# Gated cross-attention and block-sparse FFN on one core: tile 0's row maxima put into its queries by TensorE, w1's load issued without a wait, low parts of the FFN weights on GpSimd

## The reference, cut to what matters

```python
x = x + tanh(g_xattn[0]) * xattn(layernorm(x), ctx, ctx)      # 16 heads of 16, causal softmax
x = x + tanh(g_ffn[0]) * ffn(layernorm(x), w_router, b_router, w1, b1, w2, b2)

# ffn
prob = softmax(xf @ w_router + b_router); idx = top_k(prob, 4)   # mask over 16 blocks
h = relu(xf @ w1.T + b1)          # 256 -> 1024
y = (h * mask) @ w2.T + b2        # 1024 -> 256
```

## Time and profile before

| | us |
|---|---|
| median of 3 runs | 681.2 (681.01 to 684.17) |
| the profiled execution, its own time | 680.97 |
| its span in the trace | 679.1 |
| TensorE busy | 659.7 (97%) |
| GpSimd busy | 556.0 (82%) |
| ScalarE busy | 538.9 (79%) |
| VectorE busy | 527.8 (78%) |

### The profile page before, as it was taken

How to read it: one execution, slowest core, us unless ns; L and a number is a source line. 1 busy time by engine, 2 the same in 40 slices (tenths; PEclk the granted TensorE clock), 3 DMA queues, 4 the chain that set the end, 5 groups by cost and what they waited for, 6 DMA issues and landing times.

```text
span 679.1 us, 30579 instructions
## 1 busy us (share of the span) xinstructions
PE 659.7 (97%) x12960; PEld 611.9 (90%) x12960; DVE 527.8 (78%) x1429; ACT 538.9 (79%) x785; POOL 556.0 (82%) x718
## 2 busy tenths in 40 slices
PE   6779999999999999999999999999999999999997
PEld 5668899999999999999999999989999999999997
DVE  6899887788777778788778878777878877877742
ACT  4668788888888888888888888888888888887732
POOL 6677888988988898888898898888888889887643
PEclk9899999999999999999999999999999999999999
DMA  5323355556545446645556654544554554553110
GB/s 197 96 55 86 88 109 99 116 109 115 120 114 116 99 110 116 111 112 113 100 117 107 116 111 122 103 107 114 113 113 112 116 100 96 98 86 64 28 40 32
DMA packets 192279, 69.24 MB, mean 102 GB/s; under 512 B 166160, under 2 KB 191888, under 8 KB 192144
## 3 DMA queue, kind: packets, MB, share of 16 engines
q1 hardware_dynamic: 191312, 65.72, 45.7%
q10 hardware_dynamic: 832, 1.57, 0.6%
HBM read 19.03 MB, written 8.39 MB: 40 GB/s over the span
## 4 chain that ended last, share of the span: by engine, by line
PE 86%; DVE 5%; DMA 3%; ACT 2%; issue 2%; POOL 1%; SPq 1%; POOLq 0%; DVEq 0%
PE bank L423 11%; PE score_banks L344 10%; PE bank L357 8%; PE score_banks L314 8%; PE bank L425 8%; PE bank L424 8%; PE bank L446 8%; PE bank L447 8%; PE bank L448 8%; PE bank L371 4%; PE bank L401 2%; PE score_banks L327 1%; DMA used_all<-used 1%; PE bank L393 1%; ACT weights L525 1%
## 5 line engine op out<-in xcount | busy, mean ns | idle before, releaser
L880 POOL TENSOR_TENSOR h_low<-hid,h_high 128x512 fp32r<-128x512 f32 x128 | 164.2, 1283 | 12.8 <-ACT hid L560 12.8
L738 DVE SCALAR_TENSOR_TENSOR hid<-bank,b_cols,used_all 128x256 f32<-128x256 f32 x248 | 108.1, 477 | 65.9 <-PE bank L425 58.2
L873 POOL TENSOR_SCALAR_AFFINE_SELECT weights<-weights 128x1024 f32<-128x1024 f32 x128 | 138.2, 1103 | 18.2 <-ACT weights L525 16.4
L423 PE MATMUL bank<-xT_high,w_high 128*128 128x256 f32 x496 | 151.5, 305 | 0.8 <-DVE hid L738 0.7
L525 ACT ACTIVATE weights<-score_banks 128x1024 f32<-128x1024 f32 x128 | 124.3, 1024 | 34.7 <-PE score_banks L344 34.6
L424 PE MATMUL bank<-xT_low,w_high 128*128 128x256 f32 x496 | 139.4, 281 | 0.0
L425 PE MATMUL bank<-xT_high,w_low 128*128 128x256 f32 x496 | 139.4, 281 | 0.0
L446 PE MATMUL bank<-w_high,h_high 128*128 128x256 f32 x488 | 137.3, 281 | 0.7 <-POOL h_low L880 0.7
L447 PE MATMUL bank<-w_low,h_high 128*128 128x256 f32 x488 | 137.7, 282 | 0.0
L448 PE MATMUL bank<-w_high,h_low 128*128 128x256 f32 x488 | 136.2, 279 | 0.0
L423 PEld LDWEIGHTS bank<-xT_high,w_high 128*128 128x128 f32 x496 | 93.3, 188 | 8.9 <-DVE hid L738 1.1
(11 more groups left out here) (105 smaller groups left out, 1411.1 us busy)
## 6 DMA issues: line engine op xcount, KB each, us to landing
x_in<-in_x SPq DMA_DIRECT2D x31, 256.0 KB, 3.1
out_y<-y_out SPq DMA_DIRECT2D x31, 256.0 KB, 2.2
c_in<-in_ctx SPq DMA_DIRECT2D x30, 256.0 KB, 2.8
qT<-qT SPq DMA_DIRECT2D x128, 4.0 KB
w_stage<-in_w1T ACTq DMA_DIRECT2D x1, 1024.0 KB, 9.2
hid<-in_w2T SPq DMA_DIRECT2D x8, 128.0 KB, 2.7
kT_parts<-k_parts SPq DMA_TRANSPOSE x57, 2.8
qT_parts<-q_parts SPq DMA_TRANSPOSE x57, 2.7
```

What stands on the lines that cost most here:

```text
L423: pe.matmul(out=bank, lhsT=w1_high[:, k, c], rhs=high, start=k == 0, stop=False)
L738: dve.scalar_tensor_tensor(hid[:, n % 4, j], hid_bank(n)[:, j * TOKS:(j + 1) * TOKS], b1_cols[:, c:c + 1], used_all[:, p % 2], ALU.add, AL ...
L873: pool.affine_select(out=w, in_=w, compare_op=ALU.is_ge, fill=0.0, base=0, pattern=[[0, 2 * HB], [1, S]], channel_multiplier=-1).then_inc( ...
L880: pool.tensor_tensor(h_low[:, p % 2, chunks], hid[:, n % 4], h_high[:, p % 2, chunks].bitcast(F32), ALU.subtract).then_inc(h_low_made, 1)
```

## The change

For tile 0 the maxima no longer ride. VectorE writes them to a tile of their own, `first_ride` (zeroed at the start by one more memset). TensorE first copies tile 0's queries into the free bank M1 by a matmul with the identity (`first_again`, 128x512, in iteration -1), then adds the maxima into them there by eight accumulating matmuls (`first_maximum`, in iteration 0 behind scores(1)), and ScalarE copies the bank to `qT` (`first_evacuated`). `shifted_scores(0)` waits for this copy instead of the DMAs, `max_row(0)` is gone, and q_transposed(2) moves behind scores(1) and `first_maximum`. ScalarE issues w1's load without the wait for x. The pieces of the weights are made one in iteration 0, two each in 1, 2 and 3 and one in 4, and GpSimd subtracts all eight; VectorE's `weights_low` is gone.

```diff
+        first_ride = sb("first_ride", [P, HB, U, PAD], F32)
...
         def pieces_of(i):
-            return {0: (0, 1), 1: (2, 3), 2: (4, 5), 3: (6,), 4: (7,)}.get(i, ())
-        W_LOW_BY_POOL = (0, 2, 4)
+            return {0: (0,), 1: (1, 2), 2: (3, 4), 3: (5, 6), 4: (7,)}.get(i, ())
...
             def q_transposed(b):
                 pe.wait_ge(qn_made, b + 1)
-                if b >= MAX_LAG:
+                if b > MAX_LAG:
                     pe.wait_ge(max_found, b - MAX_LAG + 1)
...
+            def first_again():
+                pe.wait_ge(q_copied, 1)
+                pe.matmul(out=banks[M1][:], lhsT=ident[:], rhs=qT[:, 0, :], start=True, stop=False)
+
+            def first_maximum():
+                pe.wait_ge(max_found, 1)
+                for r in range(HB):
+                    f, t = divmod(r, 2)
+                    for g in range(2):
+                        turned = pe.matmul(out=banks[M1][:, r * S + g * HALF:r * S + (g + 1) * HALF],
+                                           lhsT=first_ride[:, 2 * t + g].rearrange("p u d -> p (u d)"),
+                                           rhs=ident[:, f * HALF:(f + 1) * HALF], start=False,
+                                           stop=r == HB - 1 and g == 1)
+                turned.then_inc(first_turned, 1)
...
             def shifted_scores(b):
-                pe.wait_ge(max_landed[s], 2 * 16 * (b // TS + 1))
+                if b == 0:
+                    pe.wait_ge(first_copied, 1)
+                else:
+                    pe.wait_ge(max_landed[s], 2 * 16 * (b // TS + (1 if s else 0)))
...
-                    pe.wait_ge(w_low_made, 2)
-                    pe.wait_ge(w_low_also_made, 2)
+                    pe.wait_ge(w_low_made, 4)
...
                     if i + 2 >= 0:
                         k_transposed(i + 2)
                         q_transposed(i + 2)
+                    if i + 1 == 0:
+                        first_again()
                 else:
-                    if q_early(i + 2):
+                    if i > 0 and q_early(i + 2):
                         q_transposed(i + 2)
...
                     if i == 0:
+                        first_maximum()
+                        q_transposed(i + 2)
                         k_transposed(i + 2)
...
+            def first_evacuated():
+                act.wait_ge(first_turned, 1)
+                act.copy(qT[:, 0, :], banks[M1][:]).then_inc(first_copied, 1)
...
-            act.wait_ge(x_landed[1], 16)
             act.dma_start(w1_stage[:].rearrange("p k e c r -> p k (e c r)"),
...
                 elif i >= 0:
+                    if i == 0:
+                        first_evacuated()
...
-                ride = q_pad[:, carrier % QS, :, RIDE_COL].rearrange("p (t g u) -> p u t g", g=2, u=U)
+                if b == 0:
+                    dve.wait_ge(first_zeroed, 1)
+                    ride = first_ride[:, :, :, MAX_COL].rearrange("p (t g) u -> p u t g", g=2)
+                else:
+                    ride = q_pad[:, carrier % QS, :, RIDE_COL].rearrange("p (t g u) -> p u t g", g=2, u=U)
...
-            def weights_low(i):
-                for n in (n for n in pieces_of(i) if n not in W_LOW_BY_POOL):
-                    _w, stage, high, low = w_piece(n)
-                    dve.wait_ge(w_high_made, n + 1)
-                    dve.tensor_tensor(low, stage, high.bitcast(F32), ALU.subtract).then_inc(w_low_also_made, 1)
...
-                    dve.wait_ge(w_low_made, 3)
-                    dve.wait_ge(w_low_also_made, 5)
+                    dve.wait_ge(w_low_made, 8)
...
+            dve.memset(first_ride[:], 0.0).then_inc(first_zeroed, 1)
...
-                weights_low(i)
                 if not early and 0 <= i - 2 < N:
...
             def weights_low(i):
-                for n in (n for n in pieces_of(i) if n in W_LOW_BY_POOL):
+                for n in pieces_of(i):
...
-                if 0 <= i < N:
+                if 1 <= i < N:
                     max_row(i)
```

More of the change, by code:

```diff
@@ L170, in build @@
         tri_made = sem("tri_made")
+        first_zeroed, first_turned, first_copied = (sem(n) for n in ("first_zeroed", "first_turned", "first_copied"))
         numbers_set, filler_set = sem("numbers_set"), sem("filler_set")
@@ L182, in build @@
             "top_found", "clipped_made", "clipped_found", "marked_made"))
-        w_low_also_made = sem("w_low_also_made")
         gated_b2_made, adding_made = sem("gated_b2_made"), sem("adding_made")
@@ L438, in ffn_out @@
                     pe.wait_ge(q_copied, QUERIES_BY_PE)
-                    pe.wait_ge(w_low_made, 3)
-                    pe.wait_ge(w_low_also_made, 5)
+                    pe.wait_ge(w_low_made, 8)
                 if t == 0:
```

## The result

688.89 us (688.21 to 690.21), against 681.95 for the kernel before in the same comparison: ratio 1.0102, interval 1.0081 to 1.0123. So the change makes the kernel 7 us slower. I had named 682.5 and a range up to 684.3. The profiled execution took 688.39 us.

A forecast was written before the change was run, and what follows sets the result against it. TensorE was taken to bound the kernel from 70 to 600 us, so a later start moves the end equally. Profiled 680.97 us plus 1.5 of router lateness, start's gain included, gave 682.5, range 680.0 to 684.3.

The forecast's parts named there:

- w1's load: ScalarE's issue at the start: from 6.58 to about 4.9 us, sharing engines with x's tiles, cost 0 to 1, taken 0.
- Rival 3: At the start, w1's load delays x's tile 4; from 0.75 us late it decides, 1.5 us gives 684.0; chance 0.07.
- the start's gain: Tile 0's second scores start at 15.3 instead of 16.07, 0.75 us; about 0.95 us ahead at iterations 1 and 2.
- the sign of being wrong: At the start, x's tile 4 landing well after 12.5 us would show the prediction wrong.
- SyncE's released loads: Loads of context, x and w2 go out from about 8.6 instead of 15.0 us; nobody needs them until iteration 2.
- The low parts: GpSimd's subtractions, 1.3 us each, ahead of roots in iterations 1 to 4 delay xn; router 0.8 to 2.2 us late, taken 1.5.
- The clock: From 17 to 21 us it should stay up, winning up to 0.5 us more, of which 0.2 was kept.
- Rival 1, 2 and 4: Start's gain survives: 680.0, chance 0.20. Hold-ups of VectorE in iterations 3, 4 add: 683.7, 0.12. Nothing net: 681.0, 0.11.
- the hold-up rival: GpSimd subtractions hold up VectorE in iterations 3 and 4: 1.5 + 0.7 + 0.5 us, 683.7; chance 0.12.

The follow-up runs named there:

- c3: Kernel before without the wait ahead of w1's load and with x's tiles 4 to 7 issued first, maxima and low parts as before: 681.75 us, ratio 0.9990.
- a2: Kernel before with only the wait ahead of w1's load taken away: 685.21 us, ratio 1.0045.
- b4: Changed kernel, w1's load still without a wait, with x's tiles 4 to 7 issued directly behind tiles 2 and 3: 684.83 us, ratio 1.0019.
- b3: Kernel before with tile 0's maxima by TensorE, SyncE waiting in iteration 0 for tile 2's query copy before later loads: 682.79 us, ratio 1.0003.
- a1: Kernel before with only tile 0's maxima put in by TensorE, w1's wait and low parts as before: 684.01 us, ratio 1.0033.
- b2: Changed kernel with TensorE's idle time filled by transposes of the identity ahead of early second scores and xn transposes: 689.82 us, ratio 1.0093.
- b1: Changed kernel with GpSimd's low parts put behind the next iteration's roots instead of ahead of them: 688.07 us, ratio 1.0077.
- c1: Changed kernel with x's tiles 4 to 7 issued first and low parts in new places, split between GpSimd and VectorE: 681.11 us, ratio 0.9988.
- c2: Changed kernel with x's tiles 4 to 7 issued first and all low parts on GpSimd behind the next iteration's roots: 682.04 us, ratio 0.9997.
- a4: Changed kernel with the wait ahead of w1's load put back: 687.27 us, ratio 1.0080.
- a3: Kernel before with only the low parts moved, all on GpSimd, one, two, two, two, one pieces: 687.34 us, ratio 1.0071.

## Why the prediction was wrong

- **w1's load: the step that failed.** I wrote that the issue would go "from 6.58 to about 4.9" and gave it "cost 0 to 1 us, I take 0". It left at 3.52, 2 us ahead of x's tiles 4 to 7. Then, not the transfer, but the issue on the other queue was held: 4.04 us for a load of 8 KB. I had priced two transfers sharing the engines, which c3 shows to cost nothing, and not one queue's issue being held by another's. The cost that I took as 0 was 3.1 us alone (a2), and the reordering that removes it from the changed kernel gives 5.7 us (b4). The Trainium skill, Perfetto Trace Analysis, DMA Instruction — HWDGE (DVE, Sync), says that the duration shown for such an issue holds first the wait for a descriptor generator that two sequencers share (it names VectorE's and SyncE's and notes that the pair is the compiler's choice; here it would be ScalarE's and SyncE's), then its use. A wait for w1's own issue doesn't fit the trace: that issue ended at 3.93, two loads of 0.1 KB went out behind its start in the usual 0.89 us (3.65 to 4.54), and the held one began at 4.58. That w1's early issue causes the hold is shown (a2 differs from before in nothing else); what in the path holds it is open. Rival 3 named the right victim, x's tile 4, with a bound of 0.75 us for losing the start's gain and a price of 684.0; the landing was 2.8 us late, which is also the sign of being wrong that I had named.
- **The start's gain: right in the trace once x is in time, in part by luck.** Predicted 0.75 us at tile 0 and 0.95 at tiles 1 and 2; b4 shows 0.7 and 1.2, b3 0.54 at tile 0 and, behind the stall, 0.7 late at tile 1. I had the second scores wait for VectorE's maxima. In b4 these ended at 14.47, as x came even earlier than before, and the second scores started at 15.35 behind TensorE's own queries and keys: `first_maximum` took 2.00 us and not 1.6. In the time no run shows this gain.
- **SyncE's released loads: wrong in general.** That "nobody needs them until iteration 2" missed that w1 shares the engines with them: a1 against b3, 2 us. In the changed kernel w1 left early enough (landed at 14.4); whether these loads slowed x's landing there, no run separates.
- **The low parts: right mechanism, sized well only at full clock.** 0.95 ahead to 1.5 behind is 2.45 us. b4 shows 1.2 ahead to 1.8 behind, 3.0. In the changed kernel it was 4.25, with TensorE idle behind xn and its clock fallen; in b2, at full clock, the same stretch is 3.3 longer than before (24.73 us). I had the wait of xn in iteration 4; the one in iteration 2 I called "level", and it was 1.57 us.
- **The clock.** I expected it to stay up from 17 to 21 us, as the idle time would be filled. It was 2.5 us of idle time again, for x instead of the maxima, and fell again. The trace of b2 puts its worth at some 2 us, its time can't tell it from nothing.
- **Rival 1, 2 and 4.** The start's gain survived in no kernel with the low parts ahead of the roots. VectorE's xn took 0.80 us at 34.95 and 51.05, beside GpSimd's x2_b2, as the hold-up rival had it, but that is 0.4 us each, not the loss; beside a low part it took 1.20 us (b1).

## What to carry to other kernels

A wait can have a second duty: the wait ahead of w1's load kept x's issue ahead of it, and the maxima's DMAs kept w2's loads behind it. Before taking one away, list what stands behind it on its queue and what on the other queues goes out in that time, and order urgent loads ahead of bulk ones by program order instead. On an in-order engine move work behind the short instruction that others wait for (here the roots), not just onto an engine with less busy time; and measure a start-up change tile by tile, since the sum of its parts tells little. And a profile is one execution: executions of the kernel before alone lie between 679.96 and 685.66 us beside c1, so a difference of 1 or 2 us between two traces needs many executions behind it.

## What was not expected of the hardware

- A load of 1 MB issued on ScalarE's queue held an issue on SyncE's for 4.04 us (after), both loads of that line for 4.22 us (a2) instead of 0.90 us. It was not the next issue but the third behind it. With x's loads ahead of it the same two loads took 1.13 us (c3), 2.08 (b4) and 2.82 (c2).
- A DMA of ScalarE's queue was issued at 3.52 us, ahead of four copies that precede it in the program (3.62 to 4.86 us).
- TensorE stalls within `attention_out(0)` until 3.2 to 3.8 us after scores(2) starts, for 0.5 to 2.2 us, or not at all (a4, b2, b4, c1).
- The clock fell, in a3 and a4, near 9 us, where the kernel before kept it with the same matmuls there; TensorE had idled 1.40 and 1.72 us just ahead, against 0.75. So executions of one program differ in it. Of the 29 executions of the kernel before beside c1, the nine with a mean granted clock of 1.00 took 681.2 us on average (679.96 to 681.89), the six with 0.992 or less 684.1 (682.93 to 685.66). Which of the two is the cause of the other, late waits or the clock, these numbers don't say.
- From tile 8 to tile 60 the traces take 522.1 us (c3) to 525.4 (b2), all at full clock and with the same work.
